# Expert weights around the hand-over from the shared expert to the routed experts: only part of them is requested before the rows

## The chip, the cores and the metric

The kernel runs on one core of a Trainium2 chip, as one program in one launch. The metric is device time in microseconds (us): the median over repeated executions. One more execution was recorded by the hardware profiler, and all rows of a trace shown here come from it. Engines: TensorE (PE: matmuls; PEld is its weight load), VectorE (DVE), ScalarE (ACT), GpSimd (POOL) and SyncE (SP), which issues DMAs. POOL issues DMAs too. The DMAs of SP travel on queue q1, those of POOL on queue q0; 16 DMA engines serve both.

## The reference

The input x is 2 x 1024 tokens of width 256, in float32. Four residual steps follow one another, each on a layer norm of x:

```python
x = x + _L0_xattn_ref(_layernorm(x), ctx, ctx, ...)   # cross attention, 16 heads, 64 keys
x = x + _L0_ffn_ref(_layernorm(x), ...)               # mixture of experts + shared expert
x = x + _L1_xattn_ref(_layernorm(x), ctx, ctx, ...)   # cross attention with biases
x = x + _L1_ffn_ref(_layernorm(x), ...)               # 8 low-rank experts, gated by batch
```

The second one matters here:

```python
scores = softmax(x_flat @ gate_w.T)                 # 8 experts
_, topk_ids = top_k(scores, 2)
g, u = split(einsum('nh,eih->nei', x_flat, experts_gate_up))   # 352 each
expert_out = einsum('nei,ehi->neh', silu(g) * u, experts_down)
out = einsum('neh,ne->nh', expert_out, w)           # w: the scores of the two chosen
shared = silu(x @ shared_gate_w.T) * (x @ shared_up_w.T) @ shared_down_w.T
out = out + sigmoid(x @ shared_expert_gate_w.T) * shared
```

## The kernel before, in words

**Stages.** Attention 0, then the shared expert (`up`, `down`, in four groups of 512 tokens), then the routed experts, then attention 1 and the last step. The shared expert ends at about 203 us of the span, the routed experts run to about 347 us.

**Precision.** A matrix product is made of three: each operand is kept as a rounded high part and the low rest. For the expert weights both are held in SBUF. The high part of gate and up (`w_hi`) is loaded early by POOL, in a form that rounds. `wd` holds per expert the low part of gate and up, and both parts of down. A low part comes about so: the full-precision weights are loaded into its place (`load_w` for gate and up, two DMAs of 352 KB an expert; `load_d(..., lo=1)` for down, three DMAs, 352 KB an expert), and `make_w_lo` or `make_d_lo` subtracts the high part in place. The high part of down is loaded by POOL (`load_d_hi(n)`: three DMAs for all the experts of group n; `D_GROUP[e]` is the group of expert e). DVE makes the low parts of experts 0 and 1, POOL those of experts 2 to 7, in their order.

**Rows.** POOL writes each token's normalised row twice into a table in device memory, at a slot sorted by expert (32 indirect DMAs of 128 rows, L1149, semaphore `scattered`). SP then fetches the table in blocks of 128 slots (`fetch(b)`, L1005, 128 KB; `fetch_tags` brings each slot's weight and destination). `xg` has NX = 4 places: block b is fetched once block b - 4 has been transposed. PE runs over NB = 39 blocks in `tensor_on`: `transpose_rows(b)`, the product with gate, that with up (`half`), then the transposes and the down product of block b - 1. The register `expert(b)` says whose weights a block needs.

**The hand-over (L1397 to L1461, L1594 to L1646).** PE's `transpose_rows(0)` stands inside the shared expert's last `down(3)`, ten matmuls ahead of its end; it waits for block 0's rows (`bx_in[0]`). After the gate product of block 0, PE waits until DVE has added all shared results to x (`sh_added`), transposes block 1, and goes on. DVE's order there: `make_w_lo(0)`, two adds, `make_w_lo(1)`, two adds, `make_d_lo(0)`, two adds, `make_d_lo(1)`, `split_rows(0)` (the low part of block 0's transposed rows), two adds, and then its loop over the blocks, whose first instruction is `split_rows(1)` and whose second is `hidden_rows(0)`.

**What SP issues there, in order (`sync_on`):** the gate and up weights of expert 0; when they have landed and the shared expert's gate products are done, those of expert 1, the down weights of experts 0 and 1 in three DMAs, gate, up and down of expert 2; then it waits for `scattered`, and fetches rows 0 to 3, tags 0, row block 4; then experts 3 to 7, with a row block after each.

**What POOL does there (`gpsimd_on`):** the 32 scatters, then `load_d_hi(0)` (experts 0 and 1), `make_w_lo(2)`, waits for `scattered`, `d_ready` 12 (the shared `down(2)` is done: its hidden parts stand where `wd` will be) and `h2_done`, `load_d_hi(1)` (experts 2 to 6), `make_d_lo(2)`, `make_w_lo(3)`, `load_d_hi(2)` (expert 7), and so on to expert 7. Only then does it begin to send the results of the blocks out (L1182).

Of the kernel before, what the change touches and what calls it, by code (L numbers as in the profile page):

```python
# [14 lines left out]
NT = B * S // P  # L15
# [10 lines left out]
KI = 3  # L26
# [648 lines left out]
def xattn_ffn_kernel(nc, x_in, ctxT_in, wq0, wk0, wv0, wo0, gate_in, egu_in, edown_in, sgate_in, sup_in, sdown_in,  # L675
                     wq1, bq1, wk1, bk1, wv1, bv1, wo1, bo1, wr_in, a_in, bw_in, out):
    ctx = ExitStack()
    with ctx:
# [7 lines left out]
        def sem(name):  # L686
            return ctx.enter_context(nc.semaphore(name))
# [270 lines left out]
        wd = here("wd", [P, E * EALL], F32R)  # L958
        of_expert = wd[:, :].rearrange("p (e n) -> p e n", e=E)
        BY_V = 2  # L960
        D_GROUP = [0, 0, 1, 1, 1, 1, 1, 2]
        w_first, d_first = sem("w_first"), sem("d_first")
        w_in = [sem(f"w_in{n}") for n in range(3)]
        weights_before = lambda e: 16 * (KD + KI) * ((e - BY_V) // 3)
        d_hi_in = [sem(f"d_hi_in{n}") for n in range(3)]

        FULL, LAST = (slice(0, P), slice(0, KI - 1)), (slice(0, IR[2]), slice(KI - 1, KI))

# [16 lines left out]
        def load_d(engine, e, end, lo, here):  # L985
            to = of_expert.bitcast(F32) if lo else of_expert
            at = EW + lo * ED
            for k in range(KI):
                engine.dma_start(to[0:IR[k], e:end, at + k * D:at + (k + 1) * D],
                                 edown_in[k * P:k * P + IR[k], e * D:end * D].rearrange("p (e n) -> p e n", e=end - e)).then_inc(here, 16)  # L990
# [44 lines left out]
        def sync_on():  # L1035
            sp = nc.sync

            for n, src in enumerate((bq1, bk1)):
                sp.dma_start(bcol[:, n, :], src.rearrange("(k p) -> p k", p=P),
                             allow_slow_non_contiguous=True).then_inc(attn1_in, 16)  # L1040
            sp.dma_start(bvrow[:, :], bv1.rearrange("(a n) -> a n", a=1)).then_inc(attn1_in, 16)
            sp.dma_start(bo_all[:, :], bo1.partition_broadcast(P)).then_inc(attn1_in, 16)

            def load_expert(e):
                wait(sp, w_in[e % 3], weights_before(e))
                load_w(sp, e, e + 1, w_in[e % 3])
                load_d(sp, e, e + 1, 1, w_in[e % 3])

            sp.wait_ge(g_ready, 3 * KS)
            load_w(sp, 0, 1, w_first)  # L1050
            sp.wait_ge(w_first, 16 * KD)
            sp.wait_ge(g_ready, 4 * KS)
            load_w(sp, 1, 2, w_first)
            load_d(sp, 0, 2, 1, d_first)
            load_expert(2)
            sp.wait_ge(scattered, 16 * 2 * NT)
            for b in range(NX):
                fetch(sp, b)
            fetch_tags(sp, 0)
            fetch(sp, NX)  # L1060
            sp.wait_ge(h2_done, len(BY_VECTOR))
            load_expert(3)
            fetch(sp, NX + 1)
            fetch_tags(sp, 1)
            sp.wait_ge(d_ready, 16)
            for e in range(4, E):
                load_expert(e)
                fetch(sp, NX + e - 2)
            fetch_tags(sp, 2)
            for b in range(NX + E - 2, 3 * NX):  # L1070
                fetch(sp, b)
            for dst, src in ((wk, wk1), (wv, wv1), (wq[1], wq1), (wo[1], wo1)):
                sp.dma_start(dst[:, :, :], split(src)).then_inc(attn1_in, 16)
            for b in range(3 * NX, NB):
                if b % TAGS == 0:
                    fetch_tags(sp, b // TAGS)
                fetch(sp, b)
# [29 lines left out]
        def gpsimd_on():  # L1107
# [46 lines left out]
            def load_d_hi(n):  # L1154
                load_d(pool, D_GROUP.index(n), D_GROUP.index(n) + D_GROUP.count(n), 0, d_hi_in[n])

            pool.wait_ge(g_ready, 4 * KS)
            load_d_hi(0)
            pool.wait_ge(w_hi_in, 16 * KD)
            for e in range(BY_V, E):  # L1160
                pool.wait_ge(lo_made, e)
                pool.wait_ge(w_in[e % 3], weights_before(e) + 16 * (KD + KI))
                make_w_lo(nc.gpsimd, e)
                if e == BY_V:
                    pool.wait_ge(scattered, 2 * 16 * NT)
                    pool.wait_ge(d_ready, 12)
                    pool.wait_ge(h2_done, len(BY_VECTOR))
                    load_d_hi(1)
                if e == BY_V + 1:
                    pool.wait_ge(d_ready, 16)  # L1170
                    load_d_hi(2)
                pool.wait_ge(d_lo_made, e)
                pool.wait_ge(d_hi_in[D_GROUP[e]], 16 * KI)
                make_d_lo(nc.gpsimd, e)

            for b in range(NB):
# [337 lines left out]
        def vector_on():  # L1514
# [111 lines left out]
                                          ALU.subtract)  # L1626
                ins.then_inc(bhL_done, 1)

            dve.wait_ge(d_hi_in[0], 16 * KI)
            dve.wait_ge(d_first, 16 * KI)  # L1630
            make_d_lo(v, 0)
            add(3, range(2))
            make_d_lo(v, 1)
            split_rows(0)
            add(3, range(2, 4))
            dve.wait_ge(sh_added, NT)
            for b in range(NB):
                if b > 0:
                    split_h(b - 1)
                if b + 1 < NB:  # L1640
                    split_rows(b + 1)
                hidden_rows(b)
                if b > 0:
                    take_y(b - 1)
# [394 lines left out]
```

## Time and profile before

| what | us |
|---|---|
| median of 3 runs | 466.02 (465.86 to 466.56) |
| the profiled execution's own time | 468.53 |
| its span in the trace | 466.8 |
| PE busy | 448.7 (96% of the span) |
| DVE / POOL / ACT busy | 306.2 / 236.5 / 209.7 |

The span runs from the first to the last instruction in the trace; the 1.7 us between it and the execution's own time lie around it. A row of the timeline is one instruction or several alike: start, duration, engine, line, operation, what it writes and reads; in brackets the time for which its engine sat idle before it, and what released it. Matmuls overlap, so the distance between the starts of two is what one costs PE, not its duration.

### The profile page before, as it was taken

How to read it: one execution, taken by the hardware profiler on the slowest of the kernel's cores; microseconds unless marked ns; L12 is line 12 of the kernel's file. 1: busy time of each engine (PE TensorE's matmuls, PEld its weight loads, DVE VectorE, ACT ScalarE, POOL GpSimd, SP SyncE). 2: the span in 40 equal slices, each digit the busy share in tenths (PEclk: the TensorE clock that was granted, in tenths of full speed). 3: DMA queues.
4: the chain of work that ended last, by engine and by line, in shares of the span. 5: the costliest groups of instructions: out<-in, count | busy, mean ns of one | idle time of the engine just before them, and what ended most of it. 6: DMA issues, size and time to landing. Idle time of an engine off the chain costs nothing.

```text
span 466.8 us, 9788 instructions
## 1 busy us (share of the span) xinstructions
PE 448.7 (96%) x3246; PEld 382.9 (82%) x3246; DVE 306.2 (66%) x683; ACT 209.7 (45%) x465; POOL 236.5 (51%) x317
## 2 busy tenths in 40 slices
PE   7999999999999999989999999999998899999997
PEld 6777777677798988989999999999977577777686
DVE  4879986676567256354555455544557679989896
ACT  3555776457714143023333333333323455776752
POOL 5323553116214767729976553333323665757645
PEclk9999999999999999989999999999999999999999
DMA  8999700000001244999923332222118200000105
GB/s 275 383 415 350 140 13 1 1 1 2 0 1 48 97 146 157 307 252 336 277 61 98 103 102 80 82 69 70 35 50 277 81 2 2 0 2 1 47 1 181
DMA packets 47921, 53.07 MB, mean 114 GB/s; under 512 B 15137, under 2 KB 42146, under 8 KB 47618
## 3 DMA queue, kind: packets, MB, share of 16 engines
q1 hardware_dynamic: 39666, 31.73, 24.0%
q0 software_dynamic: 7664, 20.19, 12.8%
q8 instruction: 29, 0.48, 0.4%
q10 hardware_dynamic: 544, 0.52, 0.3%
q14 instruction: 18, 0.15, 0.1%
HBM read 35.32 MB, written 17.12 MB: 112 GB/s over the span
## 4 chain that ended last, share of the span: by engine, by line
PE 78%; DVE 7%; ACT 4%; DMA 4%; issue 3%; POOL 2%; SPq 0%; ACTq 0%; POOLq 0%; DVEq 0%
PE banks L1317 11%; PE banks L347 6%; PE banks L1423 6%; PE banks L325 6%; PE banks L1424 5%; PE banks L1427 5%; PE banks L361 5%; PE banks L314 5%; PE banks L1372 4%; PE banks L336 3%; PE banks L1445 3%; PE banks L1449 3%; PE banks L1446 3%; PE banks L1435 3%; PE banks L1021 2%
## 5 line engine op out<-in xcount | busy, mean ns | idle before, releaser
L1625 DVE TENSOR_TENSOR hgT_lo<-banks,hgT_hi 128x256 fp32r<-128x256 f32 x78 | 24.1, 351 | 56.1 <-ACT hgT_hi L1266 56.1
L1259 ACT ACTIVATE hg<-banks 128x352 f32<-128x352 f32 x39 | 18.1, 465 | 94.5 <-PE banks L1427 94.5
L115 POOL TENSOR_TENSOR rstd<-var,mhalf 128x2 f32<-128x2 f32 x30 | 20.9, 696 | 77.2 <-DVE var L108 77.2
L1423 PE MATMUL banks<-w_hi,xgT_hi 128*128 x156 | 54.7, 351 | 0.2
L515 DVE TENSOR_REDUCE mx<-banks 128x16 f32<-128x1024 f32 x32 | 39.1, 1221 | 21.6 <-PE banks L325 21.4
L1424 PE MATMUL banks<-wd,xgT_hi 128*128 x156 | 50.3, 324 | 0.0
L1149 POOL DMA_INDIRECT expert_rows_in<-xn,slot x32 | 33.5, 1048 | 18.5 <-issue 7.7
L325 PE MATMUL banks<-kvb,qT 64*128 64x256 f32 x256 | 36.3, 401 | 1.9 <-ACT qT L433 0.6
L1427 PE MATMUL banks<-w_hi,xgT_lo 128*128 x156 | 37.6, 322 | 0.0
L125 ACT ACTIVATE xn<-x,shift,rstd 128x256 f32<-128x256 f32 x60 | 32.7, 596 | 8.1 <-POOL shift L117 7.9
L325 PEld LDWEIGHTS banks<-kvb,qT 64*128 64x128 f32 x256 | 22.5, 186 | 12.1 <-issue 8.1
L1497 DVE TENSOR_TENSOR pw<-banks,pw 128x512 f32<-128x512 f32 (+1 forms) x24 | 16.6, 691 | 23.8 <-PE banks L1317 21.0
L1317 PE MATMUL banks<-xn2T_hi,sgu_hi 128*128 128x512 f32 x80 | 31.8, 397 | 0.2 <-DVE pw L1497 0.2
L1217 ACT ACTIVATE pw<-banks 128x512 f32<-128x512 f32 (+1 forms) x24 | 14.2, 593 | 38.9 <-PE banks L1317 33.1
L1317 PE MATMUL banks<-xn2T_hi,sgu_lo 128*128 128x512 f32 x80 | 31.2, 390 | 0.0
L1317 PE MATMUL banks<-xn2T_lo,sgu_hi 128*128 128x512 f32 x80 | 31.2, 390 | 0.0
L1423 PEld LDWEIGHTS banks<-w_hi,xgT_hi 128*128 128x128 f32 x156 | 29.6, 190 | 1.5 <-issue 0.7
L1445 PE MATMUL banks<-wd,hgT_hi 128*128 (+1 forms) x117 | 29.8, 284 | 0.7 <-ACT hgT_hi L1266 0.7
L1182 POOL DMA_INDIRECT choices_out<-yy,dest x18 | 18.0, 1003 | 24.3 <-DVE yy L1618 15.2
L1446 PE MATMUL banks<-wd,hgT_hi 128*128 (+1 forms) x117 | 29.7, 283 | 0.0
L1424 PEld LDWEIGHTS banks<-wd,xgT_hi 128*128 128x128 f32 x156 | 29.7, 190 | 0.0
L314 PE MATMUL banks<-xT,wq 128*128 128x256 f32 x112 | 27.9, 392 | 0.0
(274 smaller groups left out, 1271.8 us busy)
## 6 DMA issues: line engine op xcount, KB each, us to landing
w_hi<-in_egu POOLq DMA_DIRECT2D x2, 2816.0 KB, 21.5
wd<-in_egu SPq DMA_DIRECT2D x16, 352.0 KB, 7.8
expert_rows_in<-zeros SPq DMA_DIRECT2D x1, 5304.0 KB, 40.1
xn<-expert_rows_in SPq DMA_DIRECT2D x39, 128.0 KB, 2.2
y_all<-choices_out SPq DMA_DIRECT2D x16, 256.0 KB, 4.9
out_x<-x SPq DMA_DIRECT2D x7, 256.0 KB, 2.3
x<-in_x SPq DMA_DIRECT2D x2, 768.0 KB, 8.1
wd<-in_edown SPq DMA_DIRECT2D x12, 128.0 KB, 7.9
```

The lines of the kernel that those rows point to most:

```text
L125: nc.scalar.activation(out[:, t, :], x[:, first + t, :], ACT.Identity, bias=m["shift"][:, b, t:t + 1], scale=m["rstd"][:, b, t:t + 1]).the ...
L314: last = nc.tensor.matmul(psX[:, hf, :], wq[:, k, hf * P:(hf + 1) * P], xT[:, u % 2, k, :], start=(k == 0), stop=(k == KD - 1))
L325: last = nc.tensor.matmul(psS[:, r * 512 + hf * 256:r * 512 + hf * 256 + 256], qT[rows, u % 2, hf, t * P:(t + 1) * P], kb[batch_of(u)][row ...
L347: last = nc.tensor.matmul(psO[32 * j:32 * j + 32, k, w, :], lhs, pT[u % 2][:, 4 * k + j, :], start=True, stop=True, tile_position=(0, 32 * j))
L515: nc.vector.tensor_reduce(mx, heads(psS), AX.X, ALU.max).then_inc(max_done.sem, 1)
L1149: pool.indirect_dma_start(xg_dram[:, :], bass.IndirectOffsetOnAxis(ap=slot[:, j, t:t + 1], axis=0), xn2w[:, t, :], None, bounds_check=SLOT ...
L1317: last = nc.tensor.matmul(bank[:, :], m[:, k, w * 6 * P + j * P:w * 6 * P + (j + 1) * P], v[g][:, k, :], start=(a == 0), stop=(a == len(te ...
L1423: nc.tensor.matmul(to, xgT_hi[:, c, k, :], hi, start=(k == 0), stop=False)
L1424: nc.tensor.matmul(to, xgT_hi[:, c, k, :], lo, start=False, stop=False)
L1427: last = nc.tensor.matmul(to, xgT_lo[:, c, k, :], w_hi[:, k, ds(e * (2 * I) + w * I, I)], start=False, stop=(k == KD - 1))
L1445: nc.tensor.matmul(psum[6][:, 0:D], h, d(k, 0), start=(k == 0), stop=False)
L1446: nc.tensor.matmul(psum[6][:, 0:D], h, d(k, 1), start=False, stop=False)
```

## The change

The groups of `load_d_hi` become expert 0 alone, expert 1 alone, experts 2 and 3, experts 4 to 7. Before the scatters' end SP requests only expert 1's gate and up and expert 0's down weights; after it the rows 0 to 3 come first, then expert 1's down weights, tags, and expert 2. POOL requests expert 1's and then expert 2's and 3's high down parts right after the first rows have landed, ahead of `make_w_lo(2)`. DVE makes the low part of expert 1's down weights at the end of the hand-over, after its last adds, where it now waits for both loads. `d_hi_here` holds the count that each group's semaphore reaches; groups 0 and 1 share one.

```diff
-        D_GROUP = [0, 0, 1, 1, 1, 1, 1, 2]
+        D_GROUP = [0, 1, 2, 2, 3, 3, 3, 3]
+        d_hi_here = [16 * KI, 32 * KI, 16 * KI, 16 * KI]
...
         d_hi_in = [sem(f"d_hi_in{n}") for n in range(3)]
+        d_hi_in = [d_hi_in[0], *d_hi_in]
...
             load_w(sp, 1, 2, w_first)
-            load_d(sp, 0, 2, 1, d_first)
-            load_expert(2)
+            load_d(sp, 0, 1, 1, d_first)
             sp.wait_ge(scattered, 16 * 2 * NT)
             for b in range(NX):
                 fetch(sp, b)
+            sp.wait_ge(d_first, 16 * KI)
+            load_d(sp, 1, 2, 1, d_first)
             fetch_tags(sp, 0)
+            load_expert(2)
             fetch(sp, NX)
...
             load_d_hi(0)
+            pool.wait_ge(scattered, 2 * 16 * NT)
+            pool.wait_ge(d_ready, 12)
+            pool.wait_ge(h2_done, len(BY_VECTOR))
+            pool.wait_ge(bx_in[0], 16)
+            pool.wait_ge(d_hi_in[0], d_hi_here[0])
+            load_d_hi(1)
+            load_d_hi(2)
             pool.wait_ge(w_hi_in, 16 * KD)
             for e in range(BY_V, E):
...
                 make_w_lo(nc.gpsimd, e)
-                if e == BY_V:
-                    pool.wait_ge(scattered, 2 * 16 * NT)
-                    pool.wait_ge(d_ready, 12)
-                    pool.wait_ge(h2_done, len(BY_VECTOR))
-                    load_d_hi(1)
                 if e == BY_V + 1:
                     pool.wait_ge(d_ready, 16)
-                    load_d_hi(2)
+                    load_d_hi(3)
                 pool.wait_ge(d_lo_made, e)
-                pool.wait_ge(d_hi_in[D_GROUP[e]], 16 * KI)
+                pool.wait_ge(d_hi_in[D_GROUP[e]], d_hi_here[D_GROUP[e]])
...
-            dve.wait_ge(d_hi_in[0], 16 * KI)
+            dve.wait_ge(d_hi_in[0], d_hi_here[0])
             dve.wait_ge(d_first, 16 * KI)
             make_d_lo(v, 0)
             add(3, range(2))
-            make_d_lo(v, 1)
             split_rows(0)
             add(3, range(2, 4))
             dve.wait_ge(sh_added, NT)
+            dve.wait_ge(d_hi_in[1], d_hi_here[1])
+            dve.wait_ge(d_first, 32 * KI)
+            make_d_lo(v, 1)
             for b in range(NB):
```

## Rows read from the trace of the kernel before

**Rows 1.** The chain that ended last, by engine, from the page.

```profile
PE 78%; DVE 7%; ACT 4%; DMA 4%; issue 3%; POOL 2%; SPq 0%; ACTq 0%; POOLq 0%; DVEq 0%
```

**Rows 2.** The longest wait of PE in the whole span: total, times, longest.

```profile
PE banks L1021 <- DMA xn<-expert_rows_in: 2.6, 1, 2.6
```

**Rows 3.** The chain of waits at the hand-over: start, us, what.

```profile
188.14 2.14 POOL expert_rows_in L1149
...
190.58 5.20 DMA expert_rows_in<-xn,slot
...
195.80 4.41 DMA xn<-expert_rows_in
...
200.95 2.13 PE banks L1372 x10
```

**Rows 4.** The timeline of PE there.

```profile
197.22 0.28 PE L1372 MATMUL banks<-sdn_hi,hT_lo 128*128 128x256 f32 x1
197.34 0.28 PE L1372 MATMUL banks<-sdn_hi,hT_hi 128*128 128x256 f32 x1
200.26 0.69 PE L1021 MATMUL banks<-ident,xn 128*128 128x128 f32 x2 [2.64 <-DMA xn<-expert_rows_in]
...
202.88 0.43 PE L1423 MATMUL banks<-w_hi,xgT_hi 128*128 x1
...
204.05 0.44 PE L1021 MATMUL banks<-ident,xn 128*128 128x128 f32 x2
...
206.28 0.49 PE L1435 MATMUL banks<-ident,hh 128*128 128x128 f32 x3
```

**Rows 5.** Stretches: length, busy by engine, granted clock, DMA share, GB/s.

```profile
199.70:203.10 3.40, 2.84 (x13) 2.85 (x14) 2.08 (x5) 0.38 (x1) 1.49 (x2) 0.50 0.95 195
...
205.60:220.00 14.40, 14.40 (x106) 14.19 (x105) 7.56 (x21) 4.69 (x16) 9.10 (x9) 1.00 1.14 326
```

**Rows 6.** The timeline of POOL: last scatters and the work after them.

```profile
185.12 1.06 POOL L1149 DMA_INDIRECT expert_rows_in<-xn,slot  x1 [0.30 <-issue]
186.48 1.35 POOL L1149 DMA_INDIRECT expert_rows_in<-xn,slot  x1 [0.30 <-issue]
...
190.58 0.98 POOL L1149 DMA_INDIRECT expert_rows_in<-xn,slot  x1 [0.30 <-issue]
191.56 2.21 POOL L989 DMA_DIRECT2D wd<-in_edown  x3
...
215.99 1.64 POOL L989 DMA_DIRECT2D wd<-in_edown  x3
...
238.13 1.97 POOL L1000 TENSOR_TENSOR wd<-wd 128x512 fp32r<-128x512 f32 x2
```

**Rows 7.** The timeline of SP's issues from 180 to the first row fetch.

```profile
182.62 0.84 SPq L982 DMA_DIRECT2D wd<-in_egu  x2
...
186.20 1.76 SPq L989 DMA_DIRECT2D wd<-in_edown  x3
```

**Rows 8.** Scatters: all 32, issue to landing, min/median/max.

```profile
DMA to landing us min/median/max: 2.4/2.5/7.5
```

**Rows 9.** DMAs of 256 KB of POOL issued from 190.5 to 193.2: count, KB each, median us to landing.

```profile
wd<-in_edown POOLq DMA_DIRECT2D x2, 256.0 KB, 4.8
```

**Rows 10.** The same, its DMA of 96 KB issued from 215.9 to 217.7.

```profile
wd<-in_edown POOLq DMA_DIRECT2D x1, 96.0 KB, 7.9
```

**Rows 11.** The same for the row blocks (all 39 fetches), min/median/max.

```profile
DMA to landing us min/median/max: 2.0/2.2/8.6
```

**Rows 12.** The timeline of DVE at the hand-over.

```profile
198.62 1.02 DVE L1000 TENSOR_TENSOR wd<-wd 128x512 fp32r<-128x512 f32 x2 [7.02 <-DMA wd<-in_edown]
...
203.12 0.88 DVE L1542 SCALAR_TENSOR_TENSOR x<-banks,rc_sg,x 128x256 f32<-128x256 f32 x2 [1.30 <-PE banks L1372]
205.01 0.42 DVE L1032 TENSOR_TENSOR xgT_lo<-banks,xgT_hi 128x256 fp32r<-128x256 f32 x1 [1.02 <-ACT xgT_hi L1027]
205.58 0.53 DVE L1611 TENSOR_TENSOR hh<-banks,hg 128x352 f32<-128x352 f32 x1
```

## The prediction

> **What bounds the kernel now.** I read the page's chain first: PE carries 78% of it, so time is gained where PE stands still or runs slowly [rows 1]. The waits of PE come next: the longest of the span is one of 2.6 us, for block 0's rows [rows 2]. The chain of waits shows what lies before it: a scatter instruction of 2.14 us, the last scatter, 5.20 us from its issue to its landing, and the first fetch, 4.41 us to its landing [rows 3]. The usual values of these two are 2.5 and 2.2 us [rows 8, 11]. The timeline of PE shows the stall in its place: the last matmul before it starts at 197.34, the transposes at 200.26 [rows 4]. The table of stretches shows a second price: from 199.7 to 203.1 the granted clock is 0.50, the 1.2 GHz level, and it is 1.00 (2.4 GHz) after; so it fell some 2.2 us after PE's last start [rows 5].
>
> **What is removed: the stall and the slow stretch.** At full clock the matmuls of this `down` start 0.12 us apart (197.22, 197.34 [rows 4]). Without a stall the transposes would start at 197.46 instead of 200.26: 2.80 us. From there to the first gate matmul, 202.88, PE spent 2.62 us at half clock: 2.13 on the ten matmuls [rows 3], 0.49 on the transposes. At full clock I put 1.20 and 0.22, so 198.88: another 1.20 us. The second pair of transposes, 204.05 before, also hangs on DVE's last adds, which began at 203.12 and lasted 0.88 us [rows 12]. These follow the last matmul of `down`: 198.76 + 0.28 + 0.05 = 199.09, adds done at 199.97, transposes at 200.00. The gross gain is **4.05 us**. Nothing behind this point swallows it: PE is busy 14.40 us of the next 14.40 [rows 5], and its later waits are for engines that themselves follow PE. Its bounds are 0, if the rows come as late as before, and 4.05.
>
> **Will the rows be there at 197.46?** In the old order SP puts seven parts of 352 KB on the queue between 182.6 and 188.0 [rows 7], 2,464 KB; in the new one three, 1,056 KB. A scatter takes 0.98 us and 0.30 of idle time, 1.28 in all; the gaps after 185.12 are 1.36, 1.66 and 2.44 [rows 6, 3], so 1.6 us are lost. I let 0.25 of it stay, since the first 1,056 KB still run beside them: last scatter issued at 189.2. Its landing took 5.20; the lower bound is the usual 2.5 [rows 8]; I take 3.0, nearer to that since 1.4 MB fewer are in the way: 192.2 against 195.8. First fetch: 2.2 us in the median, 4.4 before [rows 11, 3]; POOL's load beside it shrinks from 704 to 352 KB, and I take 3.0. The rows are there at **195.2**, 2.3 us ahead of need. With both upper values the issue alone still gives its 1.4 us.
>
> **What is added: a wait on DVE.** `make_d_lo(1)`, 1.02 us [rows 12], now stands between the last adds and `split_rows(1)`. As work it is free: the adds end at 199.97, and `split_rows(1)`, 205.01 before, waits for ACT and can't start before 200.96; the 1.02 us of idle time ahead of it in the old trace [rows 12] cover it. As a wait it is not free. Behind it in DVE's queue stand `split_rows(1)` and `hidden_rows(0)`, and for them wait PE's gate product of block 1 and its transposes of block 0's hidden values. PE has about 0.2 us to spare (hidden values done at 205.58 + 0.53 = 206.11 [rows 12], transposes at 206.28 [rows 4]). So each microsecond by which expert 1's down weights come after 199.97 costs PE one, less 0.2.
>
> When do they come? POOL issues the high part after the first fetch has landed, at 195.2; its own load for expert 0, issued from about 190.2, has landed by then. Three DMAs take 1.64 us to issue (POOL's load at 215.99 [rows 6]), so the third goes out at 196.3. For its landing the rows give 2.5 (POOL's quiet scatters [rows 8]), 4.8 (twice the size, at 191.6, with a backlog ahead [rows 9]) and 7.9 (96 KB under full load at 216 [rows 10]). Ahead of it at 196 are 512 KB of rows, mostly moved by then, 352 KB of expert 1's other part and the first of expert 2: more than nothing, much less than at 216. I take 4.8: **201.1**, with the ends 198.8 and 204.2. The wait then costs 201.1 - 199.97 - 0.2 = **0.95 us**; bounds 0 and 4.05. SP's part of the same weights is issued by 195.5 and is no later.
>
> A rule speaks to this number. In the old trace 96 KB of POOL's took 7.9 us near 217, in a stretch that moved 326 GB/s [rows 10, 5]: they stood behind what SP had queued. The Trainium skill ("DMA: Bandwidth & Descriptors", Queues, rings and completion order) says that each DMA engine takes the queues it has work for in turn, packet by packet. By that POOL's 352 KB would pass at half of 326 GB/s in 2.2 us, land near 199.9 and cost nothing; by the row at 216 the wait costs 4.05. The trace at 216 does not agree with an even share.
>
> **The other edits cost nothing, by this cover.** POOL now issues two groups (about 1.64 + 2.2 us) before `make_w_lo(2)`, which waits for expert 2's load, issued from about 196 instead of 185. If that lands at 206, POOL is through with `make_w_lo(2)` by 210 and with expert 7 at most 4 us after the old 240.1 (238.13 + 1.97 [rows 6]), the wait for the group of experts 4 to 7 included. The reference's router, computed on its inputs, gives the experts 2, 5, 5, 5, 7, 3, 6 and 3 blocks: expert 2 is needed at block 7, expert 3 at block 12. A block costs PE about (347 - 203) / 39 = 3.7 us, so that is near 226 and 244. POOL has 15 us to spare; if they were gone, PE would wait one for one. Results go out after 240 in both; block 14, the first that needs a buffer back, comes at 252. The bytes moved are the same. SP's new wait for `d_first` is long over when it is reached.
>
> **Sum.** 4.05 - 0.95 = 3.1 us. On the profiled execution: 468.53 - 3.1 = 465.4 (span 463.7). It ran 2.5 us above the median of the timed runs, 466.02; with the same difference off, **462.9 us**.
>
> **The rivals.**
>
> *No wait at all.* Expert 1's weights are there by 200.15 and the whole gain stays: 462.0. For it: the quiet landing of 2.5 us, and PE's own slack. Against: POOL's third DMA can't be issued before 196, and 4.8 us and more was seen with any backlog. Chance 0.23. It is also what the rule above would give.
>
> *The scatters end as late as before* (the change does not do what it says). If 1,056 KB disturb them as 2,464 did, SP fetches at 195.8; the rows land 2.2 to 2.9 us later, at 198.7. PE stands 1.25 us, too short for the clock to fall. But POOL's issue moves to 198.7, expert 1's high part lands at 199.8 + 4.8 = 204.6 against a need of 201.2, which costs 3.2 us: gain 4.05 - 1.25 - 3.2 = -0.4, 466.4. For it: the gap ahead of 188.14 is stretched by 0.4 already. Against: 1.2 of the 1.6 us are lost after 188, when the queue was longest [rows 3]. Chance 0.10.
>
> *A later row block is late.* The weights of experts 2 to 7 now all follow the first rows, some 8 MB from 195 on, and SP has issued them 4 us sooner than before, by about 215. At 326 GB/s 20 us move 6.5 MB, so up to 3 MB, or 10 us, can stand ahead of a fetch, and blocks 8 and 9 are fetched 12 to 14 us ahead of need. The worst fetch takes 8.6 us now [rows 11]. If one falls 1 to 2 us short: 464.5. Chance 0.08.
>
> *Slower: DVE's new wait outgrows the old stall.* The same mechanism as in the forecast, with the third high part landing after 204.2, the point from which the gain is eaten up. With 10 us to land it comes at 206.3: DVE waits 6.3, PE 6.1, which is 2.1 us more than is gained, and a stall of that length drops the clock again, 1.2 more: 469.3. For it: 7.9 us was seen for less data, and POOL's issue is tied to the landing of a fetch. Against: full load sets in only with expert 3's requests. Chance 0.10, of which 0.02 within the band of no change.
>
> **How the numbers follow.** My forecast has 0.49, and the time is its 462.9; alone it spans 462.0 to 464.3. The range is 461.7 to 466.0: the lower end is the whole gain with 0.3 to spare, the upper one takes in the late block and DVE waits up to 4 us; outside are most of the slower case and part of the late scatters. A change below about 0.2%, 0.9 us, can't be told from none here. Faster: 0.49 + 0.23 + 0.08 = 0.80. Same: 0.10 + 0.02 = 0.12. Slower: 0.08.
>
> **What would show it.** In the changed trace: the last scatter issued near 189.2 and landed by 192.5; no wait of PE at L1021; clock 1.00 from 195 to 210; PE's first L1423 near 198.9; DVE idle for about 1.2 us before its second L1000, released by a DMA of `in_edown`; PE idle for about 1 us in all near 202, and then unbroken. It would be wrong if PE still waits at L1021, if that DVE wait is nil or above 2.5 us, or if PE waits for weights or rows after 205.

## The result: slower, 469.2 us against 466.1

The changed kernel takes **469.2 us** in the median of 17 runs (466.94 to 472.49); the kernel before, on the same chip, 466.09 (464.96 to 467.26, 17 runs). The ratio is 1.0072, 95% interval 1.0051 to 1.0093: slower. I had forecast 462.9 with faster at 0.80. Its own runs also lie further apart than those of the kernel before: 5.6 us from lowest to highest, against 2.3.

The profiled execution took 469.27 us, its span is 467.5 and its mean clock 0.996. Lines of the code stand two to six further down than before: L1023 was L1021, L1002 was L1000, L1153 was L1149, L1433 was L1427, L1548 was L1542.

**The hand-over, PE.** The timeline of PE in the changed kernel:

```profile
197.37 0.38 PE L1023 MATMUL banks<-ident,xn 128*128 128x128 f32 x2
...
198.78 0.33 PE L1429 MATMUL banks<-w_hi,xgT_hi 128*128 x1
199.91 0.44 PE L1023 MATMUL banks<-ident,xn 128*128 128x128 f32 x2
...
203.50 0.58 PE L1433 MATMUL banks<-w_hi,xgT_lo 128*128 x2 [1.52 <-DVE xgT_lo L1034]
...
231.81 0.44 PE L1023 MATMUL banks<-ident,xn 128*128 128x128 f32 x2 [2.02 <-DMA xn<-expert_rows_in]
```

The first three rows answer to [rows 4]: block 0's rows are there in time, the transposes start at 197.37 instead of 200.26, the first gate product at 198.78 instead of 202.88, block 1's transposes at 199.91 instead of 204.05. That is the forecast (197.46, 198.88, 200.00) to 0.1 us. The other two are new: a stall of 1.52 us for DVE, and one of 2.02 for the rows of a later block. PE's longest waits after 190, in place of the one of [rows 2]:

```profile
PE banks L1023 <- DMA xn<-expert_rows_in: 2.0, 1, 2.0
PE banks L1433 <- DVE xgT_lo L1034: 1.5, 1, 1.5
```

**Where the DVE stall comes from.** POOL and DVE in the changed kernel, and POOL's 96 KB DMA issued from 197.3 to 198 (KB, us to landing):

```profile
188.04 2.14 POOL L1153 DMA_INDIRECT expert_rows_in<-xn,slot  x1 [0.30 <-issue]
190.49 0.97 POOL L1153 DMA_INDIRECT expert_rows_in<-xn,slot  x1 [0.30 <-issue]
...
196.63 3.69 POOL L991 DMA_DIRECT2D wd<-in_edown  x6 [3.46 <-DMA xn<-expert_rows_in]
```

```profile
wd<-in_edown POOLq DMA_DIRECT2D x1, 96.0 KB, 4.3
```

```profile
187.72 1.62 DVE L996 TENSOR_TENSOR wd<-wd,w_hi 128x1408 fp32r<-128x1408 f32 x1
...
198.98 0.88 DVE L1548 SCALAR_TENSOR_TENSOR x<-banks,rc_sg,x 128x256 f32<-128x256 f32 x2 [0.36 <-PE banks L1378]
202.08 1.02 DVE L1002 TENSOR_TENSOR wd<-wd 128x512 fp32r<-128x512 f32 x2 [2.23 <-DMA wd<-in_edown]
```

The scatters end 1.3 us later than I had put them: the gap ahead of the last is as long as in [rows 3, 6]. POOL begins its loads at 196.63, the third part goes out near 197.7 and lands 4.3 later, at 202.0; DVE waits 2.23 us.

**The late block and the clock.** From the chain of waits, the fetch of block 9; then stretches (length, busy by engine, granted clock, DMA share, GB/s):

```profile
220.01 11.75 DMA xn<-expert_rows_in
```

```profile
188.00:193.00 5.00, 5.00 (x44) 5.00 (x43) 2.21 (x3) 0.00 (x0) 4.66 (x5) 1.00 0.28 101
...
226.00:236.00 10.00, 7.98 (x50) 7.70 (x48) 3.91 (x10) 2.40 (x8) 2.62 (x3) 0.86 1.46 278
...
232.30:236.60 4.30, 4.30 (x21) 4.27 (x21) 1.43 (x3) 0.37 (x1) 3.22 (x3) 0.60 0.88 254
```

The same two stretches of the kernel before:

```profile
188.00:193.00 5.00, 5.00 (x44) 5.00 (x43) 2.30 (x3) 0.00 (x0) 4.55 (x4) 1.00 1.01 337
...
226.00:236.00 10.00, 10.00 (x75) 9.80 (x74) 4.97 (x14) 3.03 (x11) 10.00 (x7) 1.00 0.72 195
```

The change leaves the DMA engines at 101 GB/s for 5 us where they moved 337, which is 1.2 MB; that data comes later, and near 226 to 236 they move 278 where they moved 195. Block 9's rows, 128 KB, take 11.75 us to land, at 231.76; PE wanted them at 229.79. Behind that stall the granted clock falls: 0.60 over the next 4.3 us, so PE is at the 1.2 GHz level most of that time, and 0.40 of 4.3 is 1.7 us lost.

The 8.6 us of [rows 11] was no upper bound for the kernel before. In its second trace (e5 below) the same fetch of block 9 took 11.0 us, and nobody waited for it:

```profile
218.32 1.09 SPq L1005 DMA_DIRECT2D xn<-expert_rows_in  x1
```

```profile
xn<-expert_rows_in SPq DMA_DIRECT2D x1, 128.0 KB, 11.0
```

```profile
230.39 0.38 PE L1021 MATMUL banks<-ident,xn 128*128 128x128 f32 x2
```

The rows landed at about 229.3, and PE took them up at 230.39: 1.1 us to spare. A hand-over that brings PE 2.6 us forward would use that up by itself; the later landing (231.76 against 229.3) adds 2.4 us.

### The profile page after: what moved, and what is told of

Read it like the earlier page. It is cut to its first block, busy times and chain, and to the rows that moved or that the text cites. A ratio compares the mean times of both kernels' runs of the same rounds, so it can differ in the third digit from the quotient of the medians.

```text
span 467.5 us, 9795 instructions
## 1 busy us (share of the span) xinstructions
PE 449.2 (96%) x3246; PEld 382.8 (82%) x3246; DVE 306.2 (65%) x683; ACT 209.9 (45%) x465; POOL 237.7 (51%) x320
## 4 chain that ended last, share of the span: by engine, by line
PE 72%; DVE 7%; DMA 6%; ACT 4%; SPq 4%; issue 3%; POOL 2%; ACTq 0%; POOLq 0%; DVEq 0%
PE banks L1323 11%; PE banks L347 6%; PE banks L325 6%; PE banks L361 5%; PE banks L1429 5%; PE banks L314 5%; PE banks L1430 4%; PE banks L1433 4%; PE banks L1378 4%; PE banks L336 3%; PE banks L1451 3%; PE banks L1455 3%; PE banks L1452 3%; DMA xn<-expert_rows_in 3%; PE banks L1441 2%
## 5 line engine op out<-in xcount | busy, mean ns | idle before, releaser
L1153 POOL DMA_INDIRECT expert_rows_in<-xn,slot x32 | 33.5, 1047 | 18.5 <-issue 7.6
L1433 PE MATMUL banks<-w_hi,xgT_lo 128*128 x156 | 38.0, 325 | 1.5 <-DVE xgT_lo L1034 1.5
L1433 PEld LDWEIGHTS banks<-w_hi,xgT_lo 128*128 128x128 f32 x156 | 27.3, 189 | 1.8 <-DVE xgT_lo L1034 1.8
```

What stands on the lines that cost most here:

```text
L1153: pool.indirect_dma_start(xg_dram[:, :], bass.IndirectOffsetOnAxis(ap=slot[:, j, t:t + 1], axis=0), xn2w[:, t, :], None, bounds_check=SLOT ...
L1433: last = nc.tensor.matmul(to, xgT_lo[:, c, k, :], w_hi[:, k, ds(e * (2 * I) + w * I, I)], start=False, stop=(k == KD - 1))
```

## The experiments

**Theory F.** Two losses, each by itself larger than I had put it, eat the gain: DVE's new wait for expert 1's down weights, and a late row block after DMA work was moved from 188 to 220. Each also drops the clock in part of the executions. **Rivals:** one of the two alone; the transfers moved, whatever waits for them (then requesting expert 2 early again is the cure); or a gain that was never as large as I had read it. Each kernel ran on the same chip as the kernel before; the table gives that one's median too. The last column counts the executions whose mean granted clock was below 0.999, of all of that kernel.

| run | median us (lowest to highest) | before | ratio, 95% | clock below 0.999 |
|---|---|---|---|---|
| changed kernel | 469.20 (466.94 to 472.49) | 466.09 | 1.0072 (1.0051 to 1.0093) | 12 of 17 |
| e1_rows_first | 466.43 (464.86 to 469.87) | 465.81 | 1.0013 (0.9993 to 1.0032) | 5 of 12 |
| e2_w2_early | 468.64 (467.00 to 471.45) | 465.81 | 1.0060 (1.0033 to 1.0087) | 6 of 7 |
| e3_dlo_late | 469.24 (466.82 to 472.00) | 465.81 | 1.0085 (1.0057 to 1.0113) | 5 of 6 |
| e4_wlo_late | 468.41 (466.66 to 469.68) | 465.81 | 1.0052 (1.0037 to 1.0068) | 8 of 9 |
| e5_before_again | 465.81 (465.20 to 466.23) | 465.74 | 0.9998 (0.9988 to 1.0008) | 0 of 8 |
| e6_rows_and_dlo | 465.85 (464.55 to 468.04) | 465.74 | 1.0009 (0.9993 to 1.0025) | 2 of 11 |
| e7_before_wlo_late | 466.32 (465.17 to 469.32) | 465.74 | 1.0015 (0.9997 to 1.0033) | 2 of 12 |
| e8_before_w2_late | 467.68 (467.00 to 468.48) | 465.74 | 1.0040 (1.0025 to 1.0055) | 5 of 5 |
| e9_rows_dlo_w2 | 470.89 (468.09 to 471.96) | 475.22 | 0.9922 (0.9890 to 0.9954) | 6 of 7 |
| e10_spread_dlo | 470.23 (468.70 to 471.66) | 475.22 | 0.9920 (0.9890 to 0.9949) | 5 of 6 |
| e11_spread_dlo_w2 | 470.00 (468.25 to 476.10) | 475.22 | 0.9903 (0.9876 to 0.9930) | 11 of 12 |
| e12_spread_only | 467.98 (466.21 to 472.08) | 465.73 | 1.0062 (1.0033 to 1.0091) | 5 of 8 |
| e13_after_again | 469.45 (467.96 to 471.54) | 465.73 | 1.0071 (1.0051 to 1.0090) | 6 of 6 |
| **e14_spread_dlo_again** | **463.88 (463.07 to 464.69)** | 465.73 | **0.9962 (0.9948 to 0.9975)** | 0 of 6 |
| e15_before_spread | 465.86 (464.58 to 468.08) | 465.73 | 0.9999 (0.9990 to 1.0008) | 0 of 12 |

Runs e9 to e11 fell on another chip, on which the kernel before takes 475.22 us; only their ratios say something. The kernel before had a mean clock below 0.999 in 1 of 69 executions beside the other runs, and in 18 of 18 there.

**The row blocks ahead of the weights.**

```diff
-            load_expert(3)
             fetch(sp, NX + 1)
+            load_expert(3)
...
             for e in range(4, E):
-                load_expert(e)
                 fetch(sp, NX + e - 2)
+                load_expert(e)
```

> The changed kernel, with one reordering in SP's queue: from block 5 on each row block is requested ahead of the expert weights that it followed (block 9 no longer stands behind expert 7's weights). Theory A, the loss is a late row block: block 9's rows were requested at 220.01 us, took 11.75 us and held PE for 2.02 us, after which 1.2 GHz cost about 1.8 us more. Here block 9 can be requested when block 5 is transposed, near 215.5, and even 12 us bring it in by 228, before the need at 229.8: no wait of PE at L1023 behind block 1, and a time about 4 us or more under the 469.2 of the change, 464 to 465.5, with a small spread. Theory B, the loss is DVE's wait for expert 1's down weights (2.23 us of DVE, 1.52 of PE): it is untouched, so 468 to 470.

2.8 us below the changed kernel and level with the kernel before, as neither theory said (464 to 465.5, or 468 to 470). No row block is late in its trace. What is left is the DVE wait, longer here than in the changed kernel's own trace, and this time the clock falls behind it:

```profile
204.26 0.71 PE L1433 MATMUL banks<-w_hi,xgT_lo 128*128 x2 [2.71 <-DVE xgT_lo L1034]
```

```profile
204.00:208.00 4.00, 3.74 (x15) 3.60 (x16) 1.68 (x6) 1.28 (x4) 0.69 (x1) 0.57 1.27 303
```

Within this one kernel the median is 465.43 over the seven executions at full clock and 468.10 over the five below it. In the trace the fall itself is worth 0.43 of 4.00 us, 1.7; the other microsecond between the two medians must lie elsewhere, perhaps in longer waits, of which only the profiled execution's is seen.

**Expert 2 requested before the scatters' end again** (`load_expert(2)` moved back ahead of the wait for `scattered`).

> The changed kernel, but expert 2's three kinds of weights (1,056 KB) are requested before the scatters' end again, as in the kernel before. Theory A with its cause, a DMA gap: the changed kernel moves next to nothing from 188 to 192, and all later loads end that much later. Here 1,056 KB move in the gap, later requests are served some 3 us sooner, block 9's rows land by about 229 and PE waits there 0 to 0.5 us: 464.5 to 466.5. The scatters' last landing comes up to 1 us later than the 2.4 us of the change, the first rows still in time. Theory B: expert 1's down weights come at the same time or sooner by little: 468 or more.

The DMA engines are filled again (188 to 193, against 101 GB/s in the changed kernel), and the median hardly moves:

```profile
188.00:193.00 5.00, 5.00 (x44) 5.00 (x43) 1.68 (x3) 0.00 (x0) 4.34 (x5) 1.00 0.93 320
```

The median alone would say that the idle stretch is not the loss. The trace says more: no row block is late in it (longest landing 9.6 us), as theory A wanted, but PE's wait behind DVE is 2.6 us instead of 1.5, with the granted clock at 0.57 from 204 to 208. DVE's own wait is shorter than in the changed kernel, 1.91 us; its subtraction takes 2.45 us instead of 1.02:

```profile
201.25 2.45 DVE L1002 TENSOR_TENSOR wd<-wd 128x512 fp32r<-128x512 f32 x2 [1.91 <-DMA wd<-in_edown]
```

```profile
199.57 3.23 POOL L996 TENSOR_TENSOR wd<-wd,w_hi 128x1408 fp32r<-128x1408 f32 x1
```

Expert 2's weights now come so early that POOL subtracts for expert 2 from 199.57 to 202.80, beside DVE. So this run traded one loss for the other and can't price the idle stretch; e11 and e14 below can. The last scatter goes out no later than in the changed kernel.

**DVE's wait behind block 0's hidden values.**

```diff
-            dve.wait_ge(d_hi_in[1], d_hi_here[1])
-            dve.wait_ge(d_first, 32 * KI)
-            make_d_lo(v, 1)
             for b in range(NB):
...
                 hidden_rows(b)
+                if b == 0:
+                    dve.wait_ge(d_hi_in[1], d_hi_here[1])
+                    dve.wait_ge(d_first, 32 * KI)
+                    make_d_lo(v, 1)
```

> The changed kernel, but DVE makes the low part of expert 1's down weights after hidden_rows(0), one block later, instead of before its block loop. DVE's wait for the load then stands where DVE is idle anyway, and PE loses the 1.52 us wait at the gate product of block 1. Theory B: that and its consequences are the loss, so 465.5 to 467.5. Theory A: PE comes to block 9 1.5 us sooner, its rows come no sooner, the wait there grows by the same: 468.5 to 470, no change from 469.2.

No gain in the median, though the DVE stall is gone from its trace (of its fastest execution, 466.82 us). The wait for the late block has grown; PE's wait and the fetch, from the chain:

```profile
PE banks L1023 <- DMA xn<-expert_rows_in: 2.6, 1, 2.6
```

```profile
219.47 10.99 DMA xn<-expert_rows_in
```

PE wants block 9 1.9 us sooner than in the changed kernel (227.92 against 229.79); its rows land only 1.3 us sooner (230.46 against 231.76), and 0.6 us go into a longer wait. A stall early on pays for a part of a later one that hangs on a transfer: with two of them in a row, removing the first alone shows little.

**What stretches the last scatters.** I had blamed SP's backlog. In the trace the long ones stand beside DVE's subtractions of `make_w_lo` (L996, two operands in SBUF). Here the second subtraction follows the adds:

```diff
             add(2, range(2))
+            add(2, range(2, 4))
             dve.wait_ge(w_first, 32 * KD)
             make_w_lo(v, 1)
-            add(2, range(2, 4))
```

> The changed kernel, but DVE makes the low part of expert 1's gate and up weights after its adds at 190.6 us instead of before them at 187.7. It tells what stretches the last scatters on POOL (1.11, 1.34, 2.14 us against 0.97, the same in both kernels although 1.4 MB less were on the queues). Theory C, DVE's two subtractions of two SBUF operands hold POOL up while they overlap (185.3 to 186.9 and 187.7 to 189.3): the third stretched scatter takes 0.97 to 1.1, the last scatter is issued near 189.3 instead of 190.49, and the scatters land by 192. Theory D, the DMA queue does it: durations stay 1.3 and 2.1. The time follows theory A in either case: 468 to 470, unless the rows' earlier start takes about 1 us off.

```profile
186.41 1.35 POOL L1153 DMA_INDIRECT expert_rows_in<-xn,slot  x1 [0.30 <-issue]
188.07 0.98 POOL L1153 DMA_INDIRECT expert_rows_in<-xn,slot  x1 [0.30 <-issue]
189.35 0.97 POOL L1153 DMA_INDIRECT expert_rows_in<-xn,slot  x1 [0.30 <-issue]
```

```profile
191.44 1.61 DVE L996 TENSOR_TENSOR wd<-wd,w_hi 128x1408 fp32r<-128x1408 f32 x1
```

With the subtraction gone from 187.7 to 191.4 the scatter that took 2.14 takes 0.98, and the last goes out at 189.35 instead of 190.49; the other, still beside a subtraction, keeps its 1.35. SP's backlog is not what stretches it: it takes 2.14 us in the kernel before and in the changed one, which has 1.4 MB fewer requested by then. POOL's loads then begin at 195.37 instead of 196.63, yet PE's wait behind DVE is 2.9 us instead of 1.5. The third part, issued 1.2 us sooner, took 7.0 us to land instead of 4.3:

```profile
wd<-in_edown POOLq DMA_DIRECT2D x1, 96.0 KB, 7.0
```

So an earlier issue did not bring the weights sooner. What differs is SP's queue. In e4 SP requests expert 2 from 195.49 on, about 1 us ahead of POOL's third part; so it is in e14, e12 and e1, where that part takes 5.0, 5.3 and 5.7 us. In the changed kernel's trace it does so from 197.81 on, together with POOL's third part, because its request for the tags took 1.60 us instead of 0.43; in e3, e13 and e2, where SP's next weights go out after that part, it takes 3.4, 4.1 and 4.2 us. The order fits every trace but e10 (6.4 us, other chip); no run changes it alone, so as a cause it is not shown.

The Trainium skill ("SBUF — State Buffer", SBUF: two separate sides) says that a DVE instruction with two SBUF inputs contends with a GpSimd operation that reads SBUF, and that whichever starts first holds the shared port for the whole instruction. The rows agree: the scatter of 2.14 us ends 0.84 us after the subtraction beside it (190.18, 189.34), about what it takes alone. That the rule covers a scatter's issue is only what these rows show.

**The kernel before, once more.**

> The kernel before, unchanged, for a second trace of it. Its first profiled execution lay 2.4 us above the median of its timed ones (468.53 against 466.09), and the forecast's 4.05 us of gross gain was read from it. Theory E, that execution was a bad case: in a usual one the rows come sooner, PE waits 1 us or less at its transposes of block 0, the clock stays at 1.00 from 195 to 210, and the hand-over can give back only 1 to 2 us. Rival: the new trace shows the wait of 2.6 us and the half clock again, its own time near 466 then comes from somewhere else.

```profile
199.52 0.44 PE L1021 MATMUL banks<-ident,xn 128*128 128x128 f32 x2 [1.95 <-DMA xn<-expert_rows_in]
...
202.52 0.44 PE L1021 MATMUL banks<-ident,xn 128*128 128x128 f32 x2 [0.20 <-DVE x L1542]
```

```profile
198.00:210.00 12.00, 10.28 (x71) 9.72 (x72) 7.42 (x19) 3.58 (x11) 3.20 (x4) 1.00 1.06 260
```

In this execution, whose time (466.23) is near the median, PE waits 1.95 us instead of 2.64 (theory E said 1 or less) and the clock does not fall. Block 1's transposes start at 202.52 against 199.91 after: the gain to be had is 2.6 us, not 4.05. The chain here does not even run through the rows. It runs through POOL's load for experts 0 and 1 and DVE's subtractions and adds:

```profile
193.02 5.37 DMA wd<-in_edown
...
198.42 1.20 DVE wd L1000 x2
...
202.52 0.44 PE banks L1021 x2
```

So the rows in time would not have been enough in the old order. The execution that I had costed (468.53) was one with a fallen clock [rows 5]; of 69 later ones of this kernel 1 had a mean clock below 0.999.

**Both cures of e1 and e3 together.**

> The changed kernel with both edits of e1 (row blocks ahead of the weights they followed) and e3 (expert 1's low down part made after hidden_rows(0)). Theory F, two separate losses ate the gain, DVE's wait with the slow clock behind it (blocks 1 to 3 took 5.77 and 4.84 us in e1 against 2.45 and 3.56) and the late row block: neither alone shows in the median in full, since PE comes to the second the sooner the less it lost in the first. Together: no wait of PE over 0.5 us from 197 to 347, 461.5 to 464. Rival, theory B alone or A alone: no better than e1, 466.

```profile
PE banks L1023 <- DMA xn<-expert_rows_in: 1.9, 1, 1.9
```

```profile
222.73 12.71 DMA xn<-expert_rows_in
```

Level with the kernel before, outside the 461.5 to 464 that theory F gave, and 2.9 us below the changed one by the ratios (1.0072 - 1.0009). A block is late again, now block 10. It is fetched after expert 7's weights: moving the requests one place up moved the late place one on.

**The two parts tried on the kernel before.** e7 makes e4's edit there, e8 requests expert 2 only after tags 0.

> The kernel before, with one edit: DVE's make_w_lo(1) after the two adds that it preceded. Since e4 showed the scatter beside it fall from 2.14 to 0.98 us, the last scatter is issued 1.15 us sooner, near 189.4. If the rows' start is what the median hangs on, it falls by 1 us or a little more, to 464.8 to 465.2. If in the usual execution of the kernel before rows are not what PE waits longest for (theory E), it gains 0 to 0.5.

> The kernel before, with one part of the change alone: expert 2's weights (1,056 KB) requested after the first rows and tags instead of before the scatters' end. DVE's order and POOL's groups stay as before. Theory F: the rows come in time, nothing new waits on DVE since expert 1's down weights are still loaded early, and half of the DMA gap arises, so a late row block may or may not appear: 463.5 to 466.5. If the gap in the queues after 188 is what costs, about 468, and PE waits for a row block near 230.

Neither helps; e8 costs 1.9 us with the clock below 0.999 in all five, more than theory F allowed, and without the late row block of its rival. Its trace shows the point of e5 again: block 0's rows are in time (transposes at 197.64), but DVE's `make_d_lo(0)` still waits for its load until 198.26, PE stands 1.5 us behind the `split_rows(0)` that follows it, the granted clock is 0.60 from 202 to 206, and block 1 starts at 202.18, 0.3 us ahead of e5. In e7 the last scatter goes out at 188.74, and PE still waits 1.7 us for the rows and 2.9 us behind DVE. The trace of e7 shows the contention from the other side: DVE's `make_d_lo` took 3.32 us for the 1.02 of [rows 12] while POOL subtracted beside it, with both operands of both in SBUF:

```profile
198.43 3.32 DVE L1000 TENSOR_TENSOR wd<-wd 128x512 fp32r<-128x512 f32 x2 [5.98 <-DMA wd<-in_edown]
```

```profile
197.68 3.19 POOL L994 TENSOR_TENSOR wd<-wd,w_hi 128x1408 fp32r<-128x1408 f32 x1 [5.75 <-DMA wd<-in_edown]
```

**Pacing the row blocks by need.** The remaining fetches are spread over the weights, so that none comes after all of them:

```diff
+            fetch(sp, NX + 1)
             load_expert(3)
...
             for e in range(4, E):
+                for b in {4: (6,), 5: (7, 8), 6: (9, 10), 7: (11,)}[e]:
+                    if b == 9:
+                        fetch_tags(sp, 2)
+                    fetch(sp, b)
                 load_expert(e)
-                fetch(sp, NX + e - 2)
```

The fetches of blocks 10 and 11 behind the loop are dropped. e10 has this and e3's edit; e9 and e11 add e2's to e6 and to e10.

> e6 (the changed kernel, row blocks ahead of their weights, expert 1's low down part one block later) with e2's edit as well: expert 2's weights are requested before the scatters' end and fill the gap in the DMA queues. In e6's trace block 10's rows, still requested behind all weights, held PE for 1.9 us, and the median stayed at 465.85. Theory G, what is left is the backlog of the queues: 1,056 KB fewer stand ahead near 220, some 3 us, so block 10 comes in time and the 2.5 us that the hand-over gives (transposes of block 2 at 77.2 us behind the first shared product instead of 79.7) stay: 463 to 464.2. Rival, theory H: rows are late by the way POOL's last group (1,408 KB) shares the engines at 215 to 231, whatever was sent before: 465 to 466, a wait at block 10 or 11 again.

> The changed kernel with e3's edit and a slower pace in SP's queue: the weights of experts 5, 6 and 7 each wait until two more row blocks have been requested (rows 7 and 8 ahead of expert 5, 9 and 10 ahead of expert 6, 11 ahead of expert 7). Nothing fills the gap in the queues at 188 to 193. Theory G: no row block up to 11 stands behind more than one expert's weights and POOL's group, none is late, 463 to 464.5, no wait of PE at L1023. Theory H: POOL's group alone delays them, 465 or more. If POOL ends its low parts so late that block 14 has no place for its results, PE waits near 255 for DVE instead, and the time is 466 or more.

> e10 with expert 2's weights before the scatters' end as well. Theory G: 462.8 to 464, no later than e10, since no row is late in either; the edit then only brings POOL's work forward. If e10 still shows a late block, this one should not.

All three beat the kernel before by 0.8 to 1.0% on that chip, with intervals that overlap; expert 2's early request adds nothing that can be told. The ratios could not be carried over, so the pieces ran again on a chip on which the kernel before takes 465.73: e12 is the changed kernel with the pacing only, e13 the changed kernel, e14 the kernel of e10, e15 the kernel before with the pacing.

> The changed kernel with e10's pacing of SP's queue alone; DVE still makes expert 1's low down part before its block loop. Theory F (two losses): no late row block, but PE's wait behind DVE stays, blocks 1 to 3 take 1.5 to 4.5 us more than their 6.1: 0.3 to 1 us slower than e14 in the ratio's median at the least, about 1.000 of the kernel before. If DVE's wait costs nothing in the usual execution: as e14.

> The changed kernel, unchanged, beside the others on the same chip. Ratio to the kernel before 1.004 to 1.009 as before on a chip where that takes 466. Its trace should show one or both of the losses: a wait of PE behind DVE's xgT_lo of 1.5 to 3 us near 202, and a wait for block 9's or 10's rows of 2 us or more near 230.

> e10's kernel again, on the chip of e12, e13 and e15. Theory F: both losses are gone, the hand-over's 2.5 us remain: ratio to the kernel before 0.993 to 0.997 (462.8 to 464.5 where that takes 466), no wait of PE over 1 us from 190 to 347, and 5 to 6 us under the changed kernel. If something else ate the gain: 0.998 or more.

> The kernel before with e10's pacing alone. Its hand-over is unchanged, and no block's rows were late in its two traces (longest landing 8.6 us): ratio 0.999 to 1.001. If its usual execution had late rows too, it falls by 1 us or more.

PE's long waits after 190 in e12, then in e13:

```profile
PE banks L1433 <- DVE xgT_lo L1034: 2.3, 1, 2.3
```

```profile
PE banks L1023 <- DMA xn<-expert_rows_in: 2.2, 1, 2.2
...
PE banks L1433 <- DVE xgT_lo L1034: 1.4, 1, 1.4
```

In e14 both are gone, and the longest is one that every trace here has (0.7 us for ACT). Its waits, the start of blocks 1 and 2, and two stretches, of which the second is the whole routed part:

```profile
PE banks L1451 <- ACT hgT_hi L1272: 0.7, 1, 0.7
```

```profile
199.92 0.44 PE L1023 MATMUL banks<-ident,xn 128*128 128x128 f32 x2
...
202.48 0.38 PE L1023 MATMUL banks<-ident,xn 128*128 128x128 f32 x2
```

```profile
188.00:193.00 5.00, 5.00 (x44) 5.00 (x43) 2.21 (x3) 0.00 (x0) 4.64 (x5) 1.00 0.29 104
200.00:347.00 147.00, 146.15 (x1043) 142.08 (x1044) 76.57 (x206) 47.51 (x158) 79.86 (x100) 1.00 0.48 136
```

The same stretch of the changed kernel:

```profile
200.00:347.00 147.00, 142.58 (x1012) 139.25 (x1013) 73.52 (x196) 47.05 (x156) 78.84 (x99) 0.99 0.49 133
```

PE stands still for 147.00 - 142.58 = 4.42 us in the changed kernel and for 0.85 in e14: 3.57 us. With the 1.7 us of slow clock behind block 9 that is 5.3 of the 5.7 us between the spans (467.5 and 461.8). The medians say 5.6 (469.45 and 463.88, same chip). Theory F holds in that there are two losses: of the two cures the pacing alone gives 1.5 us (e12), the later DVE wait alone none (e3), both together 5.6.

It was wrong on how they add up. e12 was expected 0.3 to 1 us behind e14 and is 4.1 behind (467.98 and 463.88), though the two differ only in where DVE waits and no block is late in e12's trace. So DVE's wait alone costs about 4 us in the median there; by e1, the other kernel with that wait and no late block in its trace, it is 2.4 (1.0013 - 0.9962, another chip). The late block alone (e3 against e14's kernel, 1.0085 - 0.9962) costs about 5.7, and both together 5.6: they overlap. Each alone is as large as the hand-over's gain or larger. e12's trace shows 2.3 us of wait, without a fallen clock, and is of its second fastest execution (466.63); what its slower ones lose, and why e12 is behind e1, is not shown.

The idle stretch at 188 to 193 is still there in e14, at 104 GB/s, and filling it brought nothing that can be told once both cures were in (e11 against e10). The pacing brings the kernel before nothing (e15), so I put e14's gain over it, 0.38% (0.25 to 0.52%) or 1.85 us, down to the hand-over. That is less than the 2.6 of the traces; the profiled executions of e14 and e5 lie 2.7 us apart (463.53 and 466.23), one below its median and the other above.

## Why the prediction was wrong

- **The removed stall** was right in place and in time: no wait at L1023, the gate product at 198.78. Its worth was mis-sized. I made the sum on an execution with a fallen clock, and took the difference between it and the median off at the end as if it lay elsewhere; it was the very term that I was costing. Usual value: 2.6 us (e5), not 4.05. This alone puts the forecast at 464.4. I had also taken the rows for all that block 1 hung on; in e5 it hung on DVE's subtractions for experts 0 and 1, which the change happens to move forward as well.
- **"1.6 us are lost. I let 0.25 of it stay"**: all of it stayed, as in the rival to which I gave 0.10. The cause of most of it was not SP's backlog but DVE's subtraction (e4), which the change does not touch. The last scatter went out at 190.5, not 189.2, landed in 2.4 us instead of the 3.0 taken, and the rows were there at about 196.0, not 195.2: still in time, so this cost PE nothing at L1023. It also moved POOL's issue back by 1.4 us, of which 0.6 lie between the landing and the issue; but with the scatters cured the weights came no sooner (e4).
- **DVE's new wait, "0.95 us"**, is the first step that failed: the mechanism was right, the size too small. In the changed kernel's trace the landing was below what I took (4.3 us against 4.8) and the issue 1.4 late. Over all traces of the new order the landing was 3.4 to 7.0 us, by whether expert 2's weights were requested ahead of it; the quiet landing of 2.5 never came. PE's wait was 1.5 us in the changed kernel's trace, 1.4 in e13, 2.3 in e12, 2.7 in e1 and 2.9 in e4; behind the last two the clock fell too. In medians the step costs 2.4 to 4.1 us (e1 and e12 against e14), so with no late block at all the change would not have been a gain. I had let the clock fall only in the rival in which the wait is 6 us, and called a stand of 1.25 us too short for it; it fell behind one of 1.5 (e8).
- **"Nothing behind this point swallows it"** is the second. I had the late block among the rivals, with the right blocks (8 and 9) and even the right stall (1 to 2 us), but gave it 0.08 and counted it only as a reduction of an intact gain. It is in the changed kernel's trace and e13's (2.0 and 2.2 us), each time with a fallen clock behind it. I had read 8.6 us as the worst fetch; e5 shows 11.0, and 1.1 us to spare for block 9 in the old kernel, less than the gain that I was adding up. Between the traces of the changed kernel and e5, whose routed parts begin within 0.1 us, block 1 is 2.6 us ahead of the old kernel, block 8 still 0.8, and block 12 is 3.1 behind.
- **The rivals taken one by one.** Their chances were added as if only one could come. What came was two at once, a longer wait on DVE and a late block: in these two traces -2.6 (gain) + 1.8 (DVE) + 3.9 (late block, with the slow clock) = +3.1 us. The two executions lie 3.0 apart (469.27 and 466.23), the medians 3.1. The terms are those of one execution each; the runs with one cure show that either loss grows when the other is gone.
- **The cover of the other edits** held in its effect: no block waited for weights. But POOL was through with expert 7 at 250.7, 10.6 us later than before and not "at most 4".
- The best case for POOL's weights, 2.2 us from issue to landing at half of 326 GB/s, came in no trace (3.4 to 7.0). Its sum has a slip besides: 196.3 + 2.2 is 198.5, not "near 199.9". It would have cost nothing either way.

Not settled: why the chip of e9 to e11 runs the kernel before 9.5 us slower; no trace of that kernel was taken there. In the traces of all three kernels that were, PE loses time inside the shared expert's `down` to nothing that the profile shows, which no trace from the other chips has at this line (e9, PE's waits):

```profile
PE banks L1378 <- issue: 2.8, 5, 1.0
```

Why one stall drops the clock and another of the same length doesn't stays open too, and so does what e12's slower executions lose. Whether experts 4 to 7's high parts, if POOL asked for them in two groups, would shorten the late fetches of the changed kernel was not tried.

## What to carry to other kernels

A transfer moved later lands among others, and the victim is whatever small load is issued last there: list every later fetch with its time of need and its slack, from more than one trace, and take the gain off that slack too, since an earlier consumer wants its data earlier. Put it among the rivals as its own sum, not as a detail. Where two waits follow one another on a path, each cure alone shows too little, and the losses can't be added; test both together. And before costing a stall from one profiled execution, see whether its time is that of the median: where it isn't, the difference is likely to be in the stall.

## What the hardware showed that I had not expected

- Between 1.5 and 2.6 us the length of a stall of PE did not tell whether the clock falls. The granted clock fell behind waits of 1.5 (e8, 0.60 over 4 us), 2.02 (changed kernel, 0.60), 2.2 (e13), 2.6 (e2, 0.57, and the trace of [rows 5]), 2.7 (e1, 0.57) and 2.9 us (e4; e7). It stayed at 1.00 behind 1.4 (e13), 1.52 (changed kernel), 1.9 (e5, e6, e15), 2.3 (e12) and 2.6 (e3). A fall cost about 1.7 us in the traces of the changed kernel and e1. It does not explain by itself why the changed kernel's times lie so far apart: its five executions at full clock have a median of 467.64, and the eight with the same mean clock of 0.996 run from 467.20 to 472.49.
- One DVE subtraction with both inputs in SBUF stretched POOL's scatter from 0.98 to 2.14 us, and a POOL subtraction those of DVE from 1.02 to 3.32 (e7) and 2.45 (e2).
- A 128 KB row block lands 2.1 to 2.3 us after its issue in the median of each of the traces from the chips on which the kernel before takes about 466. The longest landing is 7.3 us (e15) to 13.0 (e13) by trace, and 8.6 and 11.0 in two traces of one kernel.
